# Key and query angles in one full-width product, queries moved on ScalarE, and a new order of work on all five engines

## The reference, cut to what matters

```python
key_phase   = tanh(x @ Wk + bk) * pi          # 4 sets x 8 planes = 32 columns
query_phase = tanh(x @ Wq + bq) * pi
V = x @ Wv + bv
# per set: cumsum over rows of exp(i key) * V, times conj(exp(i query)), summed over planes
total = sum_s softmax(set_weights)[s] * retrieved_s
pos_contrib = sigmoid(pos_weight) * the same with position angles
gate = sigmoid(x @ Wg + bg)
h = h + x + (gate * total + (1 - gate) * pos_contrib) / norm @ Wo + bo
# second block: top 2 of 64 experts per row (capacity 256), plus a shared expert
h = h + shared + routed
```

## Time and profile before

| | |
|---|---|
| median of 3 runs | 1766.22 us |
| profiled execution, its own time | 1764.47 us |
| its span, first to last instruction | 1762.7 us |
| busy: TensorE, VectorE, GpSimd, ScalarE | 89%, 86%, 70%, 62% |
| mean granted TensorE clock | 0.958 |
| last token product of the pair loop starts | 1406.80 us |
| last scatter starts | 1499.37 us |

### The profile page before, as it was taken

How to read it: one execution, slowest core, us unless ns; L and a number is a source line. 1 busy time by engine, 2 the same in 40 slices (tenths; PEclk the granted TensorE clock), 3 DMA queues, 4 the chain that set the end, 5 groups by cost and what they waited for, 6 DMA issues and landing times. The chain is left out here.

```text
span 1762.7 us, 34557 instructions
## 1 busy us (share of the span) xinstructions
PE 1569.5 (89%) x9606; PEld 1162.9 (66%) x9606; DVE 1511.0 (86%) x6004; ACT 1101.5 (62%) x1869; POOL 1226.0 (70%) x1162
## 2 busy tenths in 40 slices
PE   2799999999999999999999999999999982676662
PEld 1577777777777777777777777777777761455551
DVE  2589999999999999999999999999999983687761
ACT  2877777777777777777777777777777631111110
POOL 0117777777777777777777777777777777588888
PEclk9899999999999999999999999999999995798885
DMA  9866766666666666666666666666666201576653
GB/s 172 226 160 141 136 135 130 128 122 126 118 115 114 112 111 111 108 108 108 108 108 110 109 107 107 107 109 108 110 108 106 57 17 34 96 114 99 98 79 33
DMA packets 259956, 194.19 MB, mean 110 GB/s; under 512 B 65513, under 2 KB 239268, under 8 KB 259656
## 3 DMA queue, kind: packets, MB, share of 16 engines
q1 hardware_dynamic: 206008, 173.72, 52.3%
q0 software_dynamic: 51200, 17.87, 8.5%
q10 hardware_dynamic: 2576, 0.60, 0.4%
HBM read 84.84 MB, written 83.73 MB: 96 GB/s over the span
## 5 line engine op out<-in xcount | busy, mean ns | idle before, releaser
L556 POOL DMA_INDIRECT slot_rows<-xs,slot x768 | 823.6, 1072 | 219.5 <-issue 219.5
L549 POOL TENSOR_TENSOR rs<-ve,neg_half 128x6 f32<-128x6 f32 x128 | 172.0, 1343 | 245.8 <-DVE ve L1219 245.8
L615 ACT ACTIVATE img<-img 84x980 f32<-84x980 f32 (+1 forms) x192 | 341.7, 1781 | 0.5 <-DMA img<-img 0.4
L832 PE MATMUL bank<-img,w_tok 126*128 126x392 f32 (+1 forms) x640 | 224.0, 497 | 10.9 <-DMA img<-img 10.9
L596 POOL DMA_INDIRECT out_rows<-img,etok x128 | 199.5, 1559 | 29.7 <-issue 29.7
L832 PEld LDWEIGHTS bank<-img,w_tok 126*128 126x128 f32 (+1 forms) x640 | 117.9, 192 | 83.9 <-issue 13.4
L668 ACT ACTIVATE xs<-h,nb,rs 128x128 f32<-128x128 f32 x384 | 154.7, 481 | 28.5 <-DVE nb L1279 28.5
L913 PE MATMUL bank<-a_t,v 128*128 128x325 f32 (+2 forms) x768 | 167.0, 353 | 1.4 <-DVE a_t L1273 1.4
L895 PE MATMUL bank<-pos_a,v 128*128 128x325 f32 (+2 forms) x768 | 167.6, 353 | 0.0
L684 ACT ACTIVATE xh<-h,nb,rs 128x128 f32<-128x128 f32 x384 | 154.0, 482 | 3.6 <-DVE nb L1279 3.6
L913 PEld LDWEIGHTS bank<-a_t,v 128*128 128x128 f32 (+1 forms) x768 | 130.1, 190 | 28.2 <-issue 1.9
(11 more groups left out here) (192 smaller groups left out, 3669.8 us busy)
## 6 DMA issues: line engine op xcount, KB each, us to landing
img<-in_x SPq DMA_DIRECT2D x384, 150.1 KB
img<-img SPq DMA_DIRECT2D x256, 160.8 KB
img<-img SPq DMA_DIRECT2D x128, 128.6 KB
out_rows<-fin SPq DMA_DIRECT2D x128, 128.0 KB
slot_rows<-xs,slot POOLq DMA_INDIRECT x768
slot_rows<-init_rows SPq DMA_DIRECT2D x16, 540.0 KB, 5.4
img<-slot_rows SPq DMA_DIRECT2D x32, 270.0 KB, 3.3
h<-in_txt SPq DMA_DIRECT2D x64, 128.0 KB, 2.7
```

Of the source, the lines that this page charges most:

```text
L549: g.tensor_tensor(out=rs[:, q.u], in0=ve[:, q.u], in1=neg_half[:, :], op=ALU.pow).then_inc(s_rs, 1)
L556: g.indirect_dma_start(out=slots_d, out_offset=bass.IndirectOffsetOnAxis(ap=slot[0:nt, q.x, r, part:part + 1], axis=0), in_=xs[0:nt, q.x, ...
L615: a.activation(cols[:, b0:b0 + nb, :], raw[:, q.u, :].rearrange("p (t b) -> p b t", b=P)[:, b0:b0 + nb, :], ACT.Copy)\
L832: ins = mm(bank[:, 4, 0:2 * PATCHES], w_tok[r, m, :], xk[r, k.u, :, m, :], start=(m == 0), stop=(m == SHIFT - 1))
```

## The change

**One product for both angles.** `wkq` holds for the first sample the columns Wk, Wk, Wq, Wq and for the second Wq, Wq, Wk, Wk: 128 output columns each. One product per sample gives keys on one half of the partitions and queries on the other. The scores need keys and queries of a sample on the same partitions, so `moved_queries` (ScalarE, two instructions of 64 x 325) moves the queries to `qs` and multiplies them by the set weight. The row's norm moves into the mask (`maskn` in place of `mask`), and `scaled_query` leaves VectorE.

**New lists.** The bodies of all engines are ordered anew, the banks of most products differ, and many waits are dropped or merged into others, among them VectorE's waits for its own steps in the score arithmetic. TensorE does `transpose_1`, the angles, values, gates and scores of pair k-1 in body k, and the whole shared expert of pair k-3. The two `rstd` on GpSimd no longer stand together.

```diff
-for _n, _w in (("ident", 128), ("below", 128), ("mask", 2 * L), ("maskn", 2 * L), ("invn", L), ("iota", CAP),
+for _n, _w in (("ident", 128), ("below", 128), ("maskn", 2 * L), ("iota", CAP),
...
         b_col = sb("b_col", [D, 1])
         pos_t = sb("pos_t", [D, NIMG])
-        wk = sb("wk", [D, 2 * HF])
-        wq = sb("wq", [D, 2 * HF])
-        bk_col = sb("bk_col", [128, 1])
-        bq_col = sb("bq_col", [128, 1])
+        wkq = sb("wkq", [D, 2, 4 * HF])
+        bkq = sb("bkq", [128, 2])
...
-                    rstd(ve2, rs2, k.back(2), S["v_ve2"], S["p_rs2"])
+                p2 = k.back(2)
+                p3 = k.back(3)
+                p4 = k.back(4)
+                if p2.runs():
+                    rstd_2(p2)
+                if p4.runs():
+                    scatter(p4, 2)
+                    scatter(p4, 3)
                 if k.runs():
-                    rstd(ve1, rs1, k, S["v_ve1"], S["p_rs1"])
-                if k.back(4).runs():
-                    scatter(k.back(4), (1, 2, 3, 4, 5))
-                if k.back(3).runs():
-                    wait(pool, S["v_slot"], k, 3)
-                    wait(pool, S["v_meta"], k, 3)
-                    if first(k.back(3)):
-                        pool.wait_ge(s_init, 16 * (SLOTS // 1024 + 1))
-                    wait(pool, S["p_go"], k, 4)
-
-                    g.tensor_tensor(out=spare[:, 2:3], in0=neg_half[:, 0:1], in1=neg_half[:, 1:2], op=ALU.add)\
-                        .then_inc(S["p_go"], 1)
-                    scatter(k.back(3), (0,))
-
-            steps(pool, body)
+                    rstd_1(k)
+                if p4.runs():
+                    scatter(p4, 4)
+                    scatter(p4, 5)
+                if p3.runs():
+                    ready(p3)
+                    scatter(p3, 0)
+                    scatter(p3, 1)
+            steps(body, 0, 4)
 
             for u in range(2):
                 pool.wait_ge(s_store[u], 16 * NT * (PAIRS // 2))
@@ -610,11 +617,29 @@
...
                 a.activation(kq[:, k.u, :, :], ph_a[:, :, :], ACT.Sin, bias=half_pi[:, :], scale=-PI_LOW)\
                     .then_inc(S["a_sin"], 1)
 
+            def moved_queries(k):
+
+                act.wait_ge(S["a_sin"], k.count())
+                for s in range(2):
+                    to, at = slice(64 * s, 64 * s + 64), slice(64 - 64 * s, 128 - 64 * s)
+                    ins = a.activation(qs[to, k.u, :], kq[at, k.u, s, :], ACT.Identity, scale=wcol[at, 4:5])
+
...
             def body(k):
-                z, w = k.back(2), k.back(3)
+                n1 = k.back(-1)
+                p1 = k.back(1)
+                p2 = k.back(2)
+                p3 = k.back(3)
+                if p2.runs():
+                    moved_queries(p2)
+                    gate(p2)
+                if p3.runs():
...
                 for i, (t0, _) in enumerate(TILES):
                     for s in range(2):
                         r = slice(64 * s, 64 * s + 64)
-                        b = 6 - 2 * s
+                        b = (4, 6)[s]
                         dst = (bank[:, b, 0:L], bank[:, b + 1, 0:L - TILE], bank[:, b + 1, L - TILE:L])[i]
-                        ins = mm(dst, kq[r, y.u, 0, t0:t0 + TILE], qn[r, y.u, t0:L], start=(i < 2), stop=(i != 1),
+                        ins = mm(dst, kq[r, y.u, s, t0:t0 + TILE], qs[r, y.u, t0:L], start=(i < 2), stop=(i != 1),
                                  skip_group_check=True)
                 ins.then_inc(S["pe_sc"], 1)
...
-            def keys(k):
-
-                wait(pe, S["v_su"], k, 2)
-                for s in range(2):
-                    ins = mm(bank[64 * s:64 * s + 64, 6, 0:L], wk[:, :], x_t[:, s, :], start=True, stop=True)
-                ins.then_inc(S["pe_k"], 1)
-
-            def queries(k):
+            def angles_1(k):
+
+                wait(pe, S["v_h2"], k, 1)
+                mm(bank[:, 6, 0:L], wkq[:, 1, :], x_t[:, 1, :], start=True, stop=True).then_inc(S["pe_k1"], 1)
+
+            def angles_0(k):
 
                 pe.wait_ge(S["a_xt"], k.count())
-                wait(pe, S["v_su"], k, 2)
-                for s in range(2):
-                    ins = mm(bank[64 * s:64 * s + 64, 7, 0:L], wq[:, :], x_t[:, s, :], start=True, stop=True)
-                ins.then_inc(S["pe_q"], 1)
+                mm(bank[:, 5, 0:L], wkq[:, 0, :], x_t[:, 0, :], start=True, stop=True).then_inc(S["pe_k0"], 1)
 
...
             def body(k):
-                y, z, w = k.back(1), k.back(2), k.back(3)
+                p1 = k.back(1)
+                p2 = k.back(2)
+                p3 = k.back(3)
+                if p3.runs():
+                    shared_1b(p3)
+                    logits(p3)
+                    shared_1a(p3)
+                if p1.runs():
+                    transpose_1(p1)
+                if p2.runs():
+                    project(p2)
                 if k.runs():
                     token(k)
-                if first(k):
-                    position_products()
-                if y.runs():
-                    gates(y)
+                    if first(k):
+                        position_products()
+                if p3.runs():
+                    logit_rows(p3)
+                if p1.runs():
+                    angles_0(p1)
+                    angles_1(p1)
+                if p3.runs():
+                    shared_3b(p3)
+                    shared_3a(p3)
                 if k.runs():
                     token_rows(k)
-                if w.runs():
-                    shared_out(w)
-                if y.runs():
-                    scores(y)
-                if w.runs():
-                    counts(w)
-                if y.runs():
-                    position_out_0(y)
-                    phase_out_1(y)
-                    position_out_1(y)
-                if z.runs():
-                    transpose_2(z)
-                if y.runs():
-                    phase_out_0(y)
-                if z.runs():
-                    shared_3b(z)
-                    shared_1a(z)
-                    logits(z)
-                    shared_1b(z)
-                    shared_3a(z)
-                if k.runs():
-                    transpose_1(k)
-                if z.runs():
-                    logit_rows(z)
-                if y.runs():
-                    project(y)
-                if k.runs():
-                    queries(k)
-                    keys(k)
-                    values(k)
-            steps(pe, body)
+                if p1.runs():
+                    values(p1)
+                    gates(p1)
+                if p3.runs():
+                    shared_out(p3)
+                if p1.runs():
+                    position_out_1(p1)
+                    scores(p1)
+                    position_out_0(p1)
...
+            for i in range(2):
+                vv.tensor_copy(wkq[:, 1, i * 2 * HF:(i + 1) * 2 * HF], wkq[:, 0, (1 - i) * 2 * HF:(2 - i) * 2 * HF])
...
-            def scaled_query(y):
-
-                dve.wait_ge(S["a_sin"], y.count())
-                wait(dve, S["pe_sc"], y, 2)
-                TT(qn[:, y.u, :], kq[:, y.u, 1, :], wn[:, :], ALU.mult).then_inc(S["v_qn"], 1)
-
...
-            def mask(y, s, done, used):
+            def mask(y, s, done, b):
+
+                TT(a_t[:, s, :, :], bank[:, b:b + 2, 0:L],
+                   cst("maskn").rearrange("p (a l) -> p a l", a=2), ALU.mult).then_inc(S[done], 1)
+
+            def mask_0(y):
+
+                mask(y, 0, "v_ma", 4)
+
+            def mask_1(y):
 
                 dve.wait_ge(S["pe_sc"], y.count())
-                wait(dve, S[used], y, 1)
-                TT(a_t[:, s, :, :], bank[:, 6 - 2 * s:8 - 2 * s, 0:L],
-                   cst("mask").rearrange("p (a l) -> p a l", a=2), ALU.mult).then_inc(S[done], 1)
```

More of the change, by code:

```diff
@@ L119, in runs, with uses, steps, wait @@
     def runs(self):
-        return self.j is not None or 0 <= self.c < PAIRS
+        return 0 <= self.c < PAIRS
     def count(self):
-        return self.c + 1 if self.j is None else self.four + (self.c + 1)
-    def uses(self, of=2):
-        n = self.c // of + 1
-        return n if self.j is None else self.j * (4 // of) + n
-    def number(self):
-        return self.c if self.j is None else self.four + self.c
-def first(pair):
-    return pair.j is None and pair.c == 0
-SKEW = 3
-AHEAD = 3
-HEAD = 8
-TAIL0 = PAIRS - 4
-def steps(eng, body, begin=0):
-    for k in range(begin, PAIRS + SKEW + 1):
-        body(Pair(None, None, k))
-def wait(eng, sem, pair, back=0):
+        return self.c + 1
+    def uses(self, of):
+        return self.c // of + 1
+def first(pair):
+    return pair.c == 0
+def steps(body, begin, end):
+    for k in range(begin, PAIRS + end):
+        body(Pair(k))
+def wait(eng, sem, pair, back):
     q = pair.back(back)
-    if q.j is not None or 0 <= q.c < PAIRS:
+    if q.runs():
         eng.wait_ge(sem, q.count())
@@ L160, in wait_dma @@
     q = pair.back(back)
-    if q.j is not None or q.c >= 0:
+    if q.runs():
         n = len(sems)
```

(10 more changed lines are left out.)

604 lines of the change are left out of this document (291 added, 313 removed).

## The result

| | before | after |
|---|---|---|
| median of 4 runs each | 1765.73 us | 1734.83 us (1732.58 to 1737.64) |
| profiled execution, its own time | 1764.47 us | 1732.58 us |
| its span | 1762.7 us | 1729.6 us |
| third token product starts | 77.18 us | 78.55 us |
| last token product starts | 1406.80 us | 1375.89 us |

The ratio is 0.9825, with a 95% interval of 0.9805 to 0.9845: the change saves 31 us. The forecast was 1732 us.

What follows compares the result with a forecast made beforehand. TensorE was taken to bound the pair loop: -0.53 us a period over 61 periods is -32.3, with the drain's -2 all in all -34.3 us, giving 1732 us forecast; range 1716 to 1757 us.

Steps and rivals of the forecast that it cites:

- Angles, -0.40: TensorE, projection to values: 4.12 us to 3.72 a pair, 0.16 at the products, 0.12 at each passage of half width.
- Masks, -0.16: TensorE's first position and phase groups: the wait for the second mask gets hidden, gaining 0.16 us a pair.
- Values, -0.07: TensorE's gates no longer wait for VectorE's `v`, which only the positions want: 0.07 us a pair gained.
- Scores, +0.10: TensorE's half-row scores now have fp32 products on either side: one more passage, a loss of 0.10 us a pair.
- Sum: TensorE's four terms together: -0.53 us a pair, period 21.23 us, -32.3 us over 61 periods.
- VectorE: Loses `scaled_query`, 0.49 us; about 20.6 to 20.9 us a pair with idling, only 0.3 to 0.6 to spare.
- rival of a half-lost gain: VectorE idles 0.9 and not 0.6 us and loses 0.3 to TensorE waits: period 21.5, 1748 us, chance 0.13.
- ScalarE: Two added query moves take 1.05 us a pair and are hidden by about 1.1 us ahead of the scores.
- GpSimd: Scatters between the norms delay the first norm's `rstd`; 0.7 us spare at the transposes; slower rival 1795 us, chance 0.10.
- Drain, -2: After the pair loop: the go-ahead for the fourth last pair's scatters follows the last token product 2 us sooner.
- Start, 0 with 3 either way: Before the steady loop: ScalarE's later turns against a token product freed of a wait, 0 us with 3 either way.
- rival of no gain: TensorE stops elsewhere as long, as at the angles: four stops of 0.13 us, 1764 to 1768 us, chance 0.07.

Runs made afterwards that it cites:

- positions_first: The kernel after with the second position product moved ahead of the scores, leaving only the transposes of `xs` between scores and first phase product: 1759.94 us.
- half_angles: The kernel after with each of the two full-width angle products split into two of half width: 1756.24 us.
- logits_first: The kernel after with the logits' half-width products moved ahead of the shared expert's full-width one, right behind the bf16 counts: 1727.43 us.
- vector_plus: The kernel after with four more VectorE instructions that nobody needs ahead of `value_rows`: 1736.02 us in its second run.
- fused_alone: The kernel before with the fused angle products and the queries moved on ScalarE, lists, banks and waits as before: 1762.97 us, ratio 0.9973.
- fused_swaps: The kernel before with fused products, `second_rows` put ahead of `top_values` on VectorE and `columns_1` ahead of `logit_rows` on ScalarE: 1750.66 us run again.
- moves_3x: The kernel after with two more copies of each moved query on ScalarE, into a tile that nobody reads: 1778.29 us run again.
- six_between: The kernel after with six and not four scatters between the two `rstd` on GpSimd, and two fewer behind: 1814.16 us run again.

## Why the prediction was right

The time, 1732 us forecast and 1734.8 measured, and its make-up came as worked out, with the split of the largest term wrong, and the spares of VectorE and GpSimd misjudged.

- **Bound.** TensorE sets the period in both kernels. Right.
- **Angles, -0.40.** The groups from projection to values took 4.12 us and take 1.33 + 1.10 + 1.34 = 3.77; undone by itself the width costs 0.34. The mechanism is right, and the size is 0.05 less, since the groups take 1.33, 1.10 and 1.34 where I put 1.32, 1.08 and 1.32. The split is wrong: "only 0.16 is saved there" is a saving at the products, and there is none. The passages hold all of it, for they also reach into the half-width group, 0.05 at its first pair of instructions and 0.09 at its last. I had counted only what showed in the groups on either side.
- **Masks, -0.16.** Before, the first position and the first phase group took 2.44 us together; two such groups without a wait take 2.22. Of these 0.22 the part behind the counts, 0.08, has moved to `shared_1b`: 0.14 gained. Right, and `positions_first` shows that the cover is what does it. Of the 0.28 that I called too long, 0.06 was none of it: I measured by 1.08 us, and such a group takes 1.11.
- **Values, -0.07.** The gates take 1.10 and not 1.15: -0.05. Right. It is read from the rows; no run takes this wait away alone.
- **Scores, +0.10.** Before, the shared output ahead of them took 1.43 and they 1.33; now position product, scores, position product take 1.20, 1.31 and 1.20. The two neighbours together are 0.18 over twice 1.11; the shared output was 0.10 over 1.33 before; the scores are 0.02 shorter: +0.06. The loss is real, the size 0.04 too large.
- **Sum.** -0.35 - 0.14 - 0.05 + 0.06 = -0.48, against -0.49 in this pair (the 0.01 left lies in the counts and the logits' transposes) and -0.53 on average. The rest of the average is not in the steady pair: some periods of the kernel before were longer, the first ones above all, 22.6 us from the third to the fourth token product. That it came to exactly my -0.53 is luck.
- **VectorE.** 1121.71 of 1200 is 19.9 us of 21.27, less than my 20.3 to 20.9. It idles before `v` as said, and 0.2 before `a_t` and `gsets`. The rival of a half-lost gain didn't come, and 0.89 us more can be put in. VectorE is busy 0.9 us less a pair, and not only the 0.49 of `scaled_query`: the small score steps took 1.3 us one behind the other before (920.83 to 922.14 in VectorE's timeline), and now stand one by one among longer steps, where they take about 0.8. The new order and the dropped waits came together there.

  The Trainium skill, VectorE: DVE Perf Modes, The DRAIN you can't avoid, by which the dropped semaphores save nothing, had made this rival likelier. No run here took the semaphores alone away, so whether they cost anything stays open.
- **ScalarE.** The two moves take 1.15 us (1.05 forecast), their cover is 1.2 (1.1 forecast). Right.
- **GpSimd.** "I find 0.7 us to spare at the transposes": 1.7 were there, and VectorE's list, not the transposes, is where a late `rstd` first costs. The rival was a true mechanism, further off than I thought.
- **Drain, -2.** 2.6 measured, 2.2 of it at the fourth last pair's go-ahead as described. Right, by the rows; no run undoes it.
- **Start, 0 with 3 either way.** +1.37. Within what was said, but one execution says little here: in the traces of `half_angles`, `logits_first`, `positions_first` and `vector_plus`' second run, changed only inside the loop, the third token product starts at 79.5 to 81.3 us, and the fourth follows by 21.0 to 24.0. The steady period repeats to 0.01 us.

What I hadn't seen is that the change's two halves need each other. I priced the fused product by itself at 0.40 and gave the new lists 0.13. By `fused_alone` the product without the lists is worth 0.10, since the lists of before start the token product, the angles and the gates within 0.28, 0.14 and 0.12 us of the end of what they wait for (the copy of `x_t` ends at 924.98). That is my rival of no gain, at two of the places that I named for it; in the lists of the kernel after it doesn't apply.

## What to carry to other kernels

Where TensorE is full, look for products of another width or type between full-width ones: the half-width angles cost 0.34 us, and the logits, which are half as many, the same by their rows (0.09 ahead, 0.15 in the group, 0.10 behind). Computing at full width gets it back; standing behind the bf16 counts got the logits 0.08. Before a saving on the busiest engine is booked, measure at each of its waits how far behind the releaser it starts; a saving of 0.35 us was down to 0.10 where these distances were 0.12, 0.14 and 0.28. To find what an engine has to spare, put more work ahead of the wait in question: it gave at least 0.9, 1.2 and 1.7 us here, where reading the lists gave 0.3 to 0.6, 1.1 and 0.7.

## What the hardware showed that I had not expected

**A passage takes the loading of weights with it.** The cost doesn't lie in one place. In `half_angles` the last instruction before the change takes 0.09 us longer, and the first behind it 0.05 (into half width) or 0.10 (into full width). In both directions the weights are not loaded ahead (in the kernel after PEld idles 0.4 to 0.5 us before L963 and L957). That the late loading is the cause of the cost is argued, not shown.

**Late semaphores.** In the first runs of `fused_swaps`, `moves_3x`, `six_between` and `vector_plus`, one group, the kernel before took 2228.54 us in place of 1766, and the four took 2261.64, 1799.18, 2048.77 and 1784.41 us; run again they took 1750.66, 1778.29, 1814.16 and 1736.02. In the first `six_between` VectorE stood 4.6 us before the masks of one pair, for nothing that the trace names ("remote"), with the scores 4.5 us over. TensorE's timeline behind it, and the windows view of the phases:

```profile
916.56 4.70 PE L927 MATMUL bank<-a_t,v 128*128 128x325 f32 x12 [3.43 <-DVE a_t L1295]
...
916.60:921.00 4.40, 4.40 (x12) 3.56 (x13) 2.91 (x7) 2.24 (x6) 1.74 (x2) 0.50 0.02 3
```

After an idle time of 3.43 us TensorE's granted clock is 0.50 (1.2 GHz), and the phases' row has 4.70 us where the same row of the kernel after has 2.38 (943.53). So one late signal cost twice. Why the signals were late in that group stays open; run again, none of the four kernels showed a wait of that kind. The first times are not used: the 1799.18 of `moves_3x` would have matched its expected 1800 by accident.
